# Products of a zero tile in 29 places of TensorE's program, in a four-layer gated cross-attention kernel

## What is computed

```python
x = x + tanh(g_xattn[l]) * xattn_l(layernorm(x), ctx)     # l = 0..3
x = x + tanh(g_ffn[l]) * ffn_l(layernorm(x))
# xattn_l: softmax(q k^T / sqrt(8)) v, then Wo; l=2 is causal; l=3 attends for 51 chosen queries of a head
# ffn_0: gelu(x W) for the 192 rows with the highest router score, the others pass
# ffn_1: 8 experts, top 2, silu(a) * b, plus a shared expert
# ffn_2: 8 experts of width 512, top 2, gelu, plus a shared expert
# ffn_3: x and W rounded to a 6-bit grid in blocks of 32, then one product
```

## Time and profile before

| | |
|---|---|
| median of 3 runs | 957.99 us |
| the three runs | 957.99, 961.41, 955.62 us |
| span of the profiled execution | 952.6 us |
| TensorE busy in it | 873.0 us (92%) |
| DVE, ACT, POOL busy | 712.2, 639.3, 497.5 us |
| mean granted TensorE clock | 0.966 |

### The profile page before, as it was taken

One profiled execution on the slowest core, in us unless ns is written; L12 is line 12 of the kernel. 1 busy time (PEld: TensorE's weight loads), 2 busy tenths in 40 slices (PEclk: granted clock), 3 DMA queues, 4 the chain that ended last, 5 costly groups with the idle time before them and its releaser, 6 DMA issues.

```text
span 952.6 us, 22448 instructions
## 1 busy us (share of the span) xinstructions
PE 873.0 (92%) x7897; PEld 604.0 (63%) x7897; DVE 712.2 (75%) x2174; ACT 639.3 (67%) x1460; POOL 497.5 (52%) x627
## 2 busy tenths in 40 slices
PE   6798889999999999899987999999999999999963
PEld 3344347855799987478533365746588987887522
DVE  7997988878543378987998899897745357656887
ACT  2786667767774645798674767777797448777841
POOL 6446555775962234655366265557772525533172
PEclk7897999999999999999998899999999999999997
DMA  5433241221100010002102021111110010000000
GB/s 156 111 96 86 73 111 43 77 64 37 28 23 23 14 39 3 21 24 63 36 21 74 20 66 32 32 41 30 33 41 1 18 35 1 19 20 18 20 3 24
DMA packets 67519, 39.93 MB, mean 42 GB/s; under 512 B 8263, under 2 KB 65376, under 8 KB 67408
## 3 DMA queue, kind: packets, MB, share of 16 engines
q1 hardware_dynamic: 62608, 30.44, 12.5%
q0 software_dynamic: 2208, 6.78, 2.6%
q10 hardware_dynamic: 2592, 1.26, 0.5%
HBM read 11.12 MB, written 1.05 MB: 13 GB/s over the span
## 4 chain that ended last, share of the span: by engine, by line
PE 64%; DVE 16%; POOL 7%; ACT 6%; issue 5%; DMA 1%; SPq 0%; DVEq 0%; ACTq 0%; POOLq 0%
PE banks L1062 12%; PE banks L1053 12%; PE banks L886 8%; PE banks L1022 6%; DVE mx L1364 6%; PE banks L868 4%; PE banks L845 4%; PE banks L831 3%; PE banks L1032 3%; ACT probs L743 3%; POOL h L603 3%; PE banks L991 2%; PE banks L824 2%; POOL rn L650 2%; PE banks L931 2%
## 5 line engine op out<-in xcount | busy, mean ns | idle before, releaser
L1364 DVE TENSOR_REDUCE mx<-banks 128x4 f32<-128x1024 f32 (+1 forms) x240 | 284.1, 1217 | 25.9 <-PE banks L845 18.9
L743 ACT ACTIVATE probs<-banks 128x512 f32<-128x512 f32 (+1 forms) x512 | 258.7, 582 | 53.3 <-PE banks L868 50.2
L796 ACT ACTIVATE probs<-banks,b_sb 128x256 f32<-128x256 f32 x288 | 118.0, 474 | 72.8 <-PE banks L1053 71.3
L886 PE MATMUL banks<-probs,v_aug 128*9 128x256 f32 (+1 forms) x2048 | 149.1, 373 | 7.2 <-ACT probs L743 5.9
L1062 PE MATMUL banks<-w_sb,probs 128*128 128x128 f32 x1152 | 140.6, 277 | 0.2 <-ACT probs L743 0.2
L1062 PEld LDWEIGHTS banks<-w_sb,probs 128*128 128x128 f32 x1152 | 134.9, 192 | 5.7 <-issue 2.5
L1053 PE MATMUL banks<-hT,w_sb 128*128 128x256 f32 x576 | 137.4, 382 | 0.1
L596 POOL TENSOR_TENSOR rstd<-veps,mhalf 128x2 f32<-128x2 f32 x64 | 46.2, 723 | 165.5 <-DVE veps L1311 164.8
L650 POOL TENSOR_TENSOR rn<-ss,mhalf 128x32 f32<-128x32 f32 x16 | 88.0, 5500 | 53.2 <-DVE ss L1159 52.9
L1053 PEld LDWEIGHTS banks<-hT,w_sb 128*128 128x128 f32 x576 | 104.4, 190 | 14.7 <-DVE xs L1235 0.8
L845 PE MATMUL banks<-k_st,q_st 64*128 64x256 bf16 (+1 forms) x1024 | 93.4, 277 | 14.3 <-DVE mx L1364 4.6
(11 more groups left out here) (195 smaller groups left out, 1451.5 us busy)
## 6 DMA issues: line engine op xcount, KB each, us to landing
k_st<-k_parts SPq DMA_DIRECT2D x192, 64.0 KB, 2.1
q_st<-q_parts SPq DMA_DIRECT2D x186, 64.0 KB, 2.1
w_sb<-in_w POOLq DMA_DIRECT2D x16, 256.0 KB, 3.3
fc_sb<-in_fc POOLq DMA_DIRECT2D x6, 256.0 KB, 4.1
x_in<-in_x SPq DMA_DIRECT2D x8, 128.0 KB, 4.3
cT<-in_ctxT SPq DMA_DIRECT2D x8, 128.0 KB, 2.7
out_x<-xs SPq DMA_DIRECT2D x8, 128.0 KB, 2.0
q_st<-mT SPq DMA_DIRECT2D x32, 16.0 KB
```

What stands on the lines that cost most here:

```text
L743: nc.scalar.activation(probs[s][:, part % UNIT_RING, 2 * a:2 * a + 2, 0:n], b_bank(w, a + 1)[:, 0:2 * n].rearrange("p (j q) -> p j q", j=2 ...
L796: ins = nc.scalar.activation(hid[s][:, part % UNIT_RING, c, :], b_bank(w, half + 1)[:, j * ROWS:(j + 1) * ROWS], ACT.Gelu, bias=b1_sb[:, p ...
L886: ins = nc.tensor.matmul(c_bank(b, l, u // 4)[VW * i:VW * i + VR, g % 2, q0:ROWS], v_aug[s][:, t, 4 * g + i, :], probs[s][:, u % UNIT_RING ...
L1364: nc.vector.tensor_reduce(mx[s][:, r, :, hp0:hp0 + n], banks[:, first:first + 2, :].rearrange("p a (n k) -> p a n k", n=n), AX.X, ALU.max) ...
```

## The change

TensorE gets a new helper, `scratch(kind, n)`. It waits for the bank that the next step takes, and makes n products of a tile of zeros in it, each with 128 x 128 zeros held and 512 columns of zeros streamed through in bf16. The helper is called at 28 entries of the schedule, ahead of that step's own waits, with the number in the table `SCRATCH`; and in one more place, inside `("keys", 0, 0, 0)`, ahead of the product for v, with `VALUES_SCRATCH`. The numbers are 128 products together. The entries lie in the first 141 us, at 494 to 531 us and at 905 to 943 us of the profiled execution. The step's own product then overwrites the bank. The tile `zeros` is new, and DVE clears it as its first instruction; the eight products at the start use it and wait for `scratch_ready` and no longer for `zeros_ready`. No order of steps or banks changes, and nothing else is removed or moved.

```diff
--- before.py
+++ after.py
@@ -234,6 +234,18 @@
 """
 
 
+
+SCRATCH = {
+    ("turn", 1, 0, 0): 11, ("keys", 3, 0, 0): 1, ("maxima", 0, 0, 7): 1, ("maxima", 1, 0, 0): 7,
+    ("max_turn", 0, 0, 0): 6, ("attend", 0, 0, 0): 1, ("turn", 1, 4, 0): 1, ("turn", 0, 1, 0): 4,
+    ("heads", 2, 0, 0): 1, ("heads", 3, 0, 0): 1, ("heads_turn", 3, 0, 0): 2, ("heads", 0, 1, 0): 1,
+    ("heads_turn", 0, 1, 0): 3, ("attend", 1, 1, 0): 4, ("attend", 2, 1, 0): 8, ("heads_turn", 5, 0, 0): 3,
+    ("turn", 4, 1, 0): 1, ("turn", 5, 4, 0): 3, ("maxima", 4, 1, 0): 6, ("maxima", 4, 1, 1): 1,
+    ("turn", 5, 1, 0): 6, ("maxima", 6, 0, 3): 1, ("heads", 5, 3, 0): 2, ("maxima", 7, 3, 5): 4,
+    ("heads_turn", 5, 3, 0): 5, ("heads_turn", 6, 3, 0): 1, ("heads_turn", 7, 3, 0): 5, ("turn", 4, 7, 0): 31}
+VALUES_SCRATCH = 7
+
+
 class Ledger:
 
 
@@ -358,6 +370,7 @@
         iota = sb("iota", [P, EXPERTS])
         mhalf = sb("mhalf", [P, RT * HEADS])
         idle = sb("idle", [1, SLOTS, 3])
+        zeros = sb("zeros", [P, BANK // 2], BF16)
         mean_k = sb("mean_k", [P, P])
         warm = sb("warm", [1, 1])
 
@@ -419,7 +432,8 @@
         weights_loaded, columns_loaded, ident_in_place, zeros_ready, ident_ready, gbo_ready, values_loaded, gates_loaded, attn_loaded, late_loaded, w3_loaded, blk_loaded, ffn_loaded, big_loaded = (
             sem(name) for name in ("weights_loaded", "columns_loaded", "ident_in_place", "zeros_ready", "ident_ready", "gbo_ready", "values_loaded", "gates_loaded", "attn_loaded", "late_loaded", "w3_loaded",
                                    "blk_loaded", "ffn_loaded", "big_loaded"))
-        cleared_dve, cleared_pool, masks_moved = sem("cleared_dve"), sem("cleared_pool"), sem("masks_moved")
+        cleared_dve, cleared_pool, masks_moved, scratch_ready = (
+            sem(name) for name in ("cleared_dve", "cleared_pool", "masks_moved", "scratch_ready"))
         gates_done, first_ready, setup_done, w3_quantised = (
             sem(name) for name in ("gates_done", "first_ready", "setup_done", "w3_quantised"))
 
@@ -802,10 +816,10 @@
 
         @block.tensor
         def _(pe):
-            pe.wait_ge(zeros_ready, 1)
+            zeros_twice = zeros[:, :].unsqueeze(1).broadcast_to([P, 2, BANK // 2])
+            pe.wait_ge(scratch_ready, 1)
             for n in range(BANKS):
-                nc.tensor.matmul(banks[:, n, :], q_st[0][:, 0, 0:P], q_st[0][:, 0:2, :].rearrange("p h q -> p (h q)"),
-                                 start=True, stop=True)
+                nc.tensor.matmul(banks[:, n, :].rearrange("p (h q) -> p h q", h=2), zeros[:, 0:P], zeros_twice, start=True, stop=True)
             pe.wait_ge(first_ready, 1)
             set_up, late, masks, ident_loaded = False, False, False, False
 
@@ -816,6 +830,12 @@
                 if w.last_read(kind, k):
                     name, value = w.last_read(kind, k)
                     pe.wait_ge(sems[name], value)
+
+            def scratch(kind, n):
+
+                wait_bank(kind, 1)
+                for _ in range(n):
+                    nc.tensor.matmul((a_bank if kind == "a" else b_bank)(w, 1).rearrange("p (h q) -> p h q", h=2), zeros[:, 0:P], zeros_twice, start=True, stop=True)
 
             def turn_rows(k, src):
 
@@ -891,6 +911,8 @@
 
             for w.i, (step, b, l, part) in enumerate(SCHEDULE):
                 s = b % SLOTS
+                if (step, b, l, part) in SCRATCH:
+                    scratch("a" if step in ("maxima", "heads", "project", "affine3") else "b", SCRATCH[step, b, l, part])
                 if step == "keys":
                     if l == 0:
                         pe.wait_ge(sems[f"ctx_loaded{s}"], 16 * (b // SLOTS + 1))
@@ -898,6 +920,8 @@
                     nc.tensor.matmul(b_bank(w, 1)[:, 0:ROWS], wqk[:, l, 1, :], cT[s][:, :], start=True, stop=True)\
                         .then_inc(sems["b_full"], 1)
                     wait_bank("a", 1)
+                    if (b, l) == (0, 0):
+                        scratch("a", VALUES_SCRATCH)
                     if l == 0 and b < SLOTS:
                         pe.wait_ge(values_loaded, 16 * len(value_loads))
                     if l == 1 and not late:
@@ -1073,6 +1097,7 @@
 
         @block.vector
         def _(dve):
+            nc.vector.memset(zeros[:, :].bitcast(F32), 0.0).then_inc(scratch_ready, 1)
             nc.vector.memset(mhalf[:, :], -0.5)
             clear_queries(nc.vector, 0).then_inc(zeros_ready, 1)
             clear_keys(nc.vector, 0, cleared_dve)
```

## The result

| | before | after |
|---|---|---|
| median | 960.79 us (955.62 to 965.55, 11 runs) | 954.11 us (949.78 to 957.53, 11 runs) |
| span of the profiled execution | 952.6 us | 952.3 us |
| its granted clock, mean | 0.966 | 0.992 |

The ratio is 0.993, with a 95% interval of 0.9911 to 0.9949: a gain of 6.7 us. A second set gave 953.66 us (950.11 to 955.91, 10 runs) beside 960.01, ratio 0.9923 (0.9896 to 0.995).

The account below looks back on a forecast made before the run. TensorE was taken as the bound, slowed in eight half-clock stretches totalling 64.8 us. Seven stretch gains less 0.4 us for overlong products sum to 7.7 us, giving span 944.9 and time 950.3 us; range 946.5 to 957.0.

Parts of the forecast that it names:

- the rival's 954.6: Clock still falls in the opening and at 512, behind late banks: gain of only 3.4 us, 954.6 us; chance 0.14.
- the two late banks: At maxima(1,0,0) and maxima(4,1,0) the bank comes free late; if the clock falls, low ends of -1.6 and -1.9 us.
- The three of the opening: Gains for the half-clock stretches at 27.64, 75.43 and 102.74 us: 0.5, 3.0 and 0.5 us.
- 27.64, 0.5: Half-clock stretch at 27.64 us: 1.9 us possible, but DVE takes over at once; gain 0.5 us (-1.6 to 1.7).
- 75.43, 3.0: Half-clock stretch at 75.43 us: 3.7 us possible, most arrives as DVE is partly idle; gain 3.0 us (1.5 to 3.7).
- 102.74, 0.5: Half-clock stretch at 102.74 us: 1.0 us possible, but DVE is busy for nearly all; gain 0.5 us (0 to 1.0).
- 512.34 and 522.58, 2.5 together: Two half-clock stretches: 0.3 us (-1.9 to 1.2) at 512.34 with its late bank, 2.2 us (1.0 to 2.6) at 522.58.
- 911.69 and 935.59, 1.6 together: Half-clock stretches near the end: 0.7 us (0.3 to 1.5), DVE busy throughout; 0.9 us (0.5 to 1.2), only last steps shorten.
- The clock row: Rival for the whole kernel: the clock row means little, nothing to gain, products cost 0.6 us at most; 958.6 us, chance 0.03.
- The slower rival: Products at half clock outlast their waits, first the 31 ahead of the last turn: 12.0 us lost, 970.0 us; chance 0.08.
- The clock still falls in two places: Rival: falls remain in the opening and at 512, 4.3 us less gain, 954.6 us; chance 0.14.
- the absorbed rival: DVE or POOL absorbs two thirds of the gain across the stretches, leaving 2.6 us: 955.4 us; chance 0.05.

Follow-up runs that it names:

- tiny: The changed kernel with all 128 products in place, each streaming 8 columns and not 512: 961.54 us, ratio 1.0016 to the kernel before.
- again_before: The kernel before, unchanged, run again with a new profile: 961.56 us, span 959.5.
- again_after: The changed kernel, unchanged, run again with a new profile: profiled at 955.91 us, span 954.1.
- Alone the group: Of the added products only the 21 at seven entries from 494 to 531 us: 960.96 us, ratio 1.0004 to the kernel before.
- The end alone: Of the added products only the 48 at six entries from 905 us on: 956.93 us, ratio 0.9961 to the kernel before.
- mid_more: Only the products from 494 to 531 us, plus 10, 4 and 15 ahead of three attend steps between 80 and 141 us: 957.25 us, ratio 0.9958 to before.
- more_again: Second measurement of the changed kernel with 10 products ahead of attend(3,0,0) and 15, not 8, ahead of attend(2,1,0): 951.53 us, ratio 0.9911 to before.

## Why the prediction was right, and where it was wrong

It said 950.3 us, faster, and the range 946.5 to 957.0 holds the 954.1 measured. The mechanism was right: tiny and the clock of every run show it. The number came out as near as it did partly by luck, as the next two paragraphs show, and of the outcomes listed the rival's 954.6 lies nearer to 954.1 than the forecast. Its reasons (loss at the two late banks, of 1.6 and 1.9 us) are not what the traces show.

**The reference of the sum.** The forecast is 957.99, the median of three runs, less 7.7. Measured are 960.79, the median of eleven, less 6.7. So 2.8 of the 3.8 us by which it missed are the reference and 1.0 the gain. Behind that stands the step "the median of the runs is 5.4 us above the span of before; with the same distance the time is 950.3". The distance of an execution's time to its own span is 1.7 to 2.4 us, so 3.0 us and more of the 5.4 were the luck of the traced execution. The sum (7.7 us) was counted on its trace, giving a span of 944.9; the span came out at 952.3, with a gain of 0.3 against that trace. Against the median the gain is 6.7 to 7.4, since other executions of before have more falls than the traced one: about 88 us at half clock in again_before (up to DVE's last instruction), against 64.8. That 6.7 is close to 7.7 is therefore luck in part: too much was counted on the falls of the traced execution, and falls that it did not have were not counted.

**The terms.** The three of the opening make 4.0 us, where the pooled traces show 2.2; the two of the middle 2.5, where they show 1.2; the two of the end 1.6, where they show 3.5. The errors cancel.
- *27.64, 0.5:* maxima(1,0,0) did start late, at 29.95, 1.3 us behind the earlier trace rows where 0.9 was forecast. The seven products in `keys`, at half clock, held the next product back by 0.6 us (9.18 and not 8.60), though the start products had begun 1.0 us earlier; the sum has no term for this. From there to attend(0,0,0) after takes 5.7 us and before 7.1, so the term as net is 0: the two traces stand level at 35.7. In after this step was released by the transfer `q_st<-mT`, behind a wait of 0.94 us.
- *75.43, 3.0:* the step that failed: "DVE is busy for only 5.52 of 10.24 us, so most arrives". DVE was not what came next; the transfer `q_st<-mT` was. TensorE was 2.0 us ahead and the next step started 0.1 us later than before. No product had been put ahead of attend(3,0,0), since the trace of before has only 0.34 us of waiting there. In that execution half the clock had covered it; in four others without the opening's products it stands open.
- *The fall at 142 us* is in no term. The execution had none there; again_before had (145.2), and so has after, with the eight products in place and 1.99 us left open behind them. In the traces after goes from 0.5 us ahead at 136 to 2.4 behind at 150; 1.3 of it is the late transfer shown above.
- *102.74, 0.5:* the stretch is gone, and after is 0.7 us ahead of before at 112, against 0.6 behind at 97. DVE was full there and yet about 1.3 arrived, over the high end of 1.0.
- *512.34 and 522.58, 2.5 together:* the stage gets 2.0 us shorter in after, when both stretches are away, and nothing in again_after. Alone the group gives -0.4 us (-2.8 to 1.9). Over all traces it is 1.2 us. The size was nearly right for an execution that holds the clock (2.0 in five of seven traces), and the step that took this for every execution was wrong. The late bank cost what was said: the six products hold L865 back by 1.40 us from the bank's release, where 1.30 were counted.
- *911.69 and 935.59, 1.6 together:* undersized. The end alone gives 3.7 us (2.1 to 5.4). The second term (0.9) was right, 1.0 in the traces. The first was read off an execution with 3.4 us at half clock there, and again_before has 10.2 between 916 and 931.

**The price of a product** was right: 0.216 us against 0.215. At half clock it is 0.42 (the seven in `keys`, and the six of again_after). The cover was as said: 31 products leave 1.40 us of the 8.08.

**The rivals.** The clock row means what it says: L1015 x8 takes 1.97 us at 0.50 and 1.09 us at 1.00 in after too, and tiny turns the whole gain off. So the caveat that the prediction cites from the Trainium skill, "TensorE: Matmul & The Clock Gate", section on the clock gate, doesn't bear on this case. The same section's figure of under 1% is for warming up; what was gained here by avoiding falls all through the kernel, 0.7 to 0.9%, lies under it too. The slower rival needed products at half clock from the start; zeros hold the clock, and mid_more and again_after show its price at one place each, and the seven in `keys` did, in the first 9.3 us. "The clock still falls in two places" came true in the sense that it falls in three: at 19, 81 and 142 us in after, and at 82, 144 and 523 in again_after, where only the last is a place that the rival named. A share of the absorbed rival did too: 2.0 us at 81, to a transfer and not to DVE or POOL.

**The signs it named.** The mean clock (0.992 for 0.99) and the 31 products (6.85 us, ended before POOL's release) came as said. "No stretch at 0.50 behind 60 us except perhaps one at 512" and "eight L991 transposes near 1.1 us everywhere" did not: there are stretches at 80.6 and 142.0, and the transposes at 142.75 take 1.97 us. Of the signs of being wrong none showed in after; in more_again the clock does fall soon behind the 31 products, at 945.6.

## What to carry to other kernels

- A trace is one execution. Where the granted clock falls at different waits in different executions, compare the trace's time with the kernel's own runs (its span plus the usual distance, here 1.7 to 2.4 us) and take two or three traces of before; price the falls that the kernel can have, not those of one trace.
- Products without a use, put into waits that another engine ends, are worth what the half clock behind the wait would cost. At half clock a product takes twice as long (0.42 to 0.43 and not 0.216 us), and a number that just fits at the full clock then holds the next step back, as in mid_more. And look again after the change: where TensorE is faster, a wait can open that half the clock had covered, as at 81 us.
- Shorter waits in front of dense work can be worth more than the longest wait of the kernel, behind which little is left to do: here 2.4 us for 17 products, and 0.8 us for 31.

## What the runs showed of the hardware

- The clock stays up through products of zeros: 31 of them, 6.85 us at 1.00, and 62, 13.54 us. With 8 columns in the same instructions the mean clock of the runs is 0.956 to 0.968, as without any.
- The same program, waits and data lose the clock at different places in different executions: half clock for 64.8 and 88 us in two of before, and at 522.6 in one of two of after. The Trainium skill, "TensorE: Matmul & The Clock Gate", section on the clock gate, calls the number of slow products at a kernel's start variable from run to run; these traces show the same in the middle and at the end.
- The clock also falls among waits of 0.53 to 0.74 us (522.6 in again_after). In after the same three waits (0.53, 0.57, 0.73 us) pass at the full clock. What decides there is open.
- SP's issue of one DMA of `q_st<-q_parts` took 0.60 us in most cases and 1.85 in one of six ahead of 137 us in after. The transfer behind it was issued 1.4 us behind its data. What lengthens it is open.
